# A fused stage with a one-group TensorE loop and single buffers, and row sums written for every row of O in layer 0

## The reference, cut to what matters

```python
def _attn(q_in, k_in, v_in, wq, bq, wk, bk, wv, bv, wo, bo, causal):
    Q = (q_in @ wq + bq).reshape(Bq, Sq, H, HD)
    Kp = (k_in @ wk + bk).reshape(Bq, Sk, H, HD)
    V = (v_in @ wv + bv).reshape(Bq, Sk, H, HD)
    scores = jnp.einsum('bqhd,bkhd->bhqk', Q, Kp) / jnp.sqrt(jnp.float32(HD))
    ...
    a = jax.nn.softmax(scores, axis=-1)
    o = jnp.einsum('bhqk,bkhd->bqhd', a, V).reshape(Bq, Sq, Dm)
    return o @ wo + bo
...
x = _layernorm(x + _attn(x, x, x, ..., True), ln1_g, ln1_b)                             # "sa"
x = _layernorm(x + _attn(x, encoder_output, encoder_output, ..., False), ln2_g, ln2_b)  # "ca"
x = _layernorm(x + _moe(x, ...), ln3_g, ln3_b)
# layer 1: attention of _layer_norm(x) over _layer_norm(context), x + out, then the MLP
```

## Time and profile before

| | |
|---|---|
| three runs | 1499.0, 1501.34, 1504.86 us (median 1501.34) |
| the profiled execution | 1501.08 us, span 1499.4 us |
| layers sa and ca | about 14 to 560 us |
| routing, experts | to about 944 us |
| fused stage | about 947 to 1357 us |
| MLP | to the end |
| PE busy / granted clock over the span | 86% / 0.933 of full speed |

### The profile page before, as it was taken

One profiled execution on the slowest core, in us unless ns is written; L12 is line 12 of the kernel. 1 busy time (PEld: TensorE's weight loads), 2 busy tenths in 40 slices (PEclk: granted clock), 3 DMA queues, 4 the chain that ended last, 5 costly groups with the idle time before them and its releaser, 6 DMA issues. The chain is left out here.

```text
span 1499.4 us, 59843 instructions
## 1 busy us (share of the span) xinstructions
PE 1284.4 (86%) x23136; PEld 1073.3 (72%) x23136; DVE 969.2 (65%) x2107; ACT 997.0 (66%) x2030; POOL 861.9 (57%) x1340
## 2 busy tenths in 40 slices
PE   5999999989999987679999999157887777895998
PEld 2787887778888776568999999136665556683776
DVE  4787787767878865883555555266877767762332
ACT  1778877768788852986666666166776666772554
POOL 2557766656676753108999987566555554322331
PEclk9999999999999995598999999669999999996999
DMA  3232332322322430522222223242332323212221
GB/s 102 76 103 91 98 105 91 95 87 80 89 80 88 117 90 8 176 64 63 69 68 68 68 67 65 66 106 65 84 89 68 96 64 82 66 31 57 71 70 49
DMA packets 154923, 118.91 MB, mean 79 GB/s; under 512 B 17440, under 2 KB 130592, under 8 KB 154784
## 3 DMA queue, kind: packets, MB, share of 16 engines
q1 hardware_dynamic: 146336, 99.61, 22.6%
q0 software_dynamic: 8448, 17.32, 5.1%
HBM read 78.55 MB, written 38.27 MB: 78 GB/s over the span
## 5 line engine op out<-in xcount | busy, mean ns | idle before, releaser
L831 DVE TENSOR_REDUCE at_mx<-at_ps_s 128x16 f32<-128x1024 f32 x128 | 156.1, 1220 | 106.9 <-PE at_ps_s L560 60.4
L760 ACT ACTIVATE at_pt<-at_ps_t 128x1024 f32<-128x1024 f32 x128 | 130.6, 1020 | 56.3 <-PE at_ps_t L574 55.6
L753 ACT ACTIVATE at_pr<-at_dd 128x1024 f32<-128x1024 f32 x128 | 135.2, 1056 | 34.7 <-DVE at_dd L839 34.6
L2261 ACT ACTIVATE ex_hg<-ex_ps_h,ex_wt 128x128 f32<-128x128 f32 x544 | 154.4, 372 | 1.3 <-PE ex_ps_y L2230 1.2
L2201 POOL DMA_INDIRECT ex_xg<-x,ex_ti x136 | 141.2, 1038 | 23.4 <-issue 21.8
L2282 DVE COPY ex_wt<-experts 128x1156 f32 x136 | 105.0, 774 | 75.7 <-issue 64.3
L839 DVE TENSOR_TENSOR at_dd<-at_ps_s,at_mx 128x1024 f32<-128x1024 f32 x128 | 153.8, 1203 | 0.1
L2221 PE MATMUL ex_ps_h<-ex_xt,ex_wt 128*128 128x128 f32 x1088 | 148.6, 281 | 0.0
L1611 POOL DMA_INDIRECT l_yg<-rows,l_sl x128 | 128.8, 1007 | 33.0 <-issue 30.8
L574 PE MATMUL at_ps_t<-ident,at_pr 128*128 128x128 f32 x1024 | 139.9, 280 | 5.1 <-issue 3.1
L2230 PE MATMUL ex_ps_y<-ex_wt,ex_hg 128*128 128x128 f32 x1088 | 143.6, 275 | 0.4 <-ACT ex_hg L2261 0.4
(11 more groups left out here) (239 smaller groups left out, 3282.9 us busy)
## 6 DMA issues: line engine op xcount, KB each, us to landing
rows<-ex_y SPq DMA_DIRECT2D x136, 64.0 KB
x<-at_ln_out SPq DMA_DIRECT2D x32, 256.0 KB, 3.2
at_kx<-in_xt SPq DMA_DIRECT2D x16, 256.0 KB, 2.8
at_qx<-in_xt SPq DMA_DIRECT2D x16, 256.0 KB, 2.8
at_vin<-in_xt SPq DMA_DIRECT2D x16, 256.0 KB, 2.7
at_xr<-in_x SPq DMA_DIRECT2D x16, 256.0 KB, 3.0
x1t<-at_xt SPq DMA_DIRECT2D x16, 256.0 KB, 3.2
at_kx<-in_ctxt SPq DMA_DIRECT2D x16, 256.0 KB, 2.7
```

The costliest lines, as they stand in the source:

```text
L753: act.activation(pr[:, p], dd[:, p], ACT.Exp, scale=SCALE).then_inc(p_ready, 1)
L760: act.activation(pt[:, 2 * h + p], ps_t[:, :, :, :], ACT.Copy).then_inc(pt_ready, 1)
L831: dve.tensor_reduce(mx[:, p], ps_s[:, :, 4 * p:4 * p + 4, :], AX.X, ALU.max).then_inc(mx_ready, 1)
L2261: ins = act.activation(hg[:, s % 2, f, :], ps_h[s % HB][:, f, :], ACT.Gelu, bias=wt[:, s % HB, B1 + f:B1 + f + 1])
```

## The change

In `attention_phase`, `values` now multiplies by `c.count_all`, a block with ones for every row of a head, and writes the sums of sequence b beside its O, to columns 256 + 64 b onward. All 256 columns come out as row sums, and DVE inverts all of them and multiplies O by them straight from PSUM. `copy_o`, `spread` and `widen` are gone there, with their tiles and semaphores. `fused_phase` keeps `recip` of 64 columns, `spread`, `copy_o` and `widen`.

In `fused_phase` the PE program runs `over_ones`, a loop over one group (groups 2 to 14), and `kv`, `qx`, `kb`, `qb`, `c.vx`, `ot`, `z4` have one buffer each; `kv` is split into `kx` and `vin`, loaded apart. PE projects k one group ahead, and v in the group's own step, ahead of the next group's first scores. The orders on PE, ACT, DVE, POOL and SP are turned so that a step starts at another place, and a few neighbours are exchanged.

```diff
@@ attention_phase @@
-        rc = n.sb("rc", [P, 2, SEQ])
-        rcx = n.sb("rcx", [P, 2, QB, SEQ])
-        ov = n.sb("ov", [P, 2, GT // 2])
+        rc = n.sb("rc", [P, 2, GT // 2])
...
                             for r in range(4):
-                                mm = pe.matmul(ps_o[32 * r:32 * r + 32, GT // 2:GT // 2 + SEQ],
-                                               c.count[:, b, f, :],
+                                mm = pe.matmul(ps_o[32 * r:32 * r + 32,
+                                                    GT // 2 + SEQ * b:GT // 2 + SEQ * b + SEQ],
+                                               c.count_all[:, 24 * f:24 * f + 32],
                                                pt[:, 2 * h + b // 2, b % 2, r, SEQ * f:SEQ * f + SEQ],
                                                start=False, stop=(b == QB - 1 and f == 1), skip_group_check=True)
...
-                    if prior:
-                        widen(g * 2 - 2, 0)
...
-                    if prior:
-                        copy_o(g * 2 - 2, 0)
...
                 def recip(quad, h):
                     dve.wait_ge(pv_ready, quad + 1)
-                    if beyond(quad, 1):
-                        dve.wait_ge(rcx_ready, quad - 1)
-                    dve.reciprocal(rc[:, h, :], ps_o[:, GT // 2:GT // 2 + SEQ]).then_inc(rc_ready, 1)
+                    dve.reciprocal(rc[:, h, :], ps_o[:, GT // 2:GT]).then_inc(rc_ready, 1)
 
                 def normalise(a, h):
                     quad = a.g * 2 + h
-                    dve.wait_ge(r_ready, quad + 1)
+                    dve.wait_ge(rc_ready, quad + 1)
                     if beyond(a.g, 0):
                         dve.wait_ge(o_ready, a.g)
-                    dve.wait_ge(ov_ready, quad + 1)
-                    dve.tensor_tensor(ot[:, GT // 2 * h:GT // 2 * h + GT // 2], ps_o[:, GT // 2:GT], ov[:, h, :],
+                    dve.tensor_tensor(ot[:, GT // 2 * h:GT // 2 * h + GT // 2], ps_o[:, 0:GT // 2], rc[:, h, :],
                                       ALU.mult).then_inc(ot_ready, 1)
...
-                    if prior:
-                        spread(g * 2 - 2, 0)
@@ fused_phase @@
-        kv = n.sb("kv", [P, 2, GT])
-        qx = n.sb("qx", [P, 2, GT])
+        kx = n.sb("kx", [P, GT])
+        vin = n.sb("vin", [P, GT])
+        qx = n.sb("qx", [P, GT])
...
                 def step(a):                                   # SP
-                    if a.shift(2).exists():
-                        load_kv(a.shift(2))
                     if a.shift(1).exists():
                         load_x(a.shift(1))
                     if a.shift(-2).exists():
                         store_tok(a.shift(-2))
-                    if a.shift(5).exists():
-                        load_front(a.shift(5))
+                    if a.shift(4).exists():
+                        load_front(a.shift(4))
                     if a.shift(3).exists():
                         store_x3(a.shift(3))
+                    if a.shift(2).exists():
+                        load_k(a.shift(2))
+                    if a.shift(1).exists():
+                        load_v(a.shift(1))
...
-                over_steps(pe, step, NG - 2)
+                over_ones(pe, step, -1, NG - 1, NG + 2)
...
                 def mask_k(a):
                     act.wait_ge(k_ready, a.g + 1)
-                    if beyond(a.g, 1):
-                        act.wait_ge(s_ready, 2 * a.g - 2)
+                    if beyond(a.g, 0):
+                        act.wait_ge(s_ready, 2 * a.g)
```

More of the change, by code:

```diff
@@ L597, in values @@
                     mm.then_inc(pv_ready, 1)
[L599 to L603, removed]
                 def project_k(a):
@@ L955, in mask_q @@
                     ins.then_inc(qb_ready, 1)
[L957 to L960, removed]
-                    pool.tensor_tensor(rcx[:, h], rc[:, h, None, :].broadcast_to([P, QB, SEQ]),
-                                       c.own[:, :, None].broadcast_to([P, QB, SEQ]), ALU.mult).then_inc(rcx_ready, 1)
                 def add_bias(a):
@@ L1006, in _ @@
                 last = At(nl, NG * nl - 1)
-                spread(last.g * 2, 0)
                 if closing:
@@ L1010, in _ @@
                     gain(last.shift(-1))
-                spread(last.g * 2 + 1, 1)
                 context.pool_rstd(pool, c, 0, 0)
@@ L1087, in fused_phase @@
         z4t_ready, qx_ready = n.sem("z4t_ready"), n.sem("qx_ready")
-        in_kv = [n.sem(f"in_kv{i}") for i in range(2)]
+        in_k, in_v = n.sem("in_k"), n.sem("in_v")
         in_x = [n.sem(f"in_x{i}") for i in range(2)]
@@ L1219, in project_k @@
                 def project_k(a):
-                    pe.wait_ge(in_kv[a.u], 16 * (a.k + 1))
-                    pe.matmul(ps_g[:, :], layer.wk[:, :], kv[:, a.u, :], start=True, stop=True).then_inc(
+                    pe.wait_ge(in_k, 16 * a.g + 16)
+                    pe.matmul(ps_g[:, :], layer.wk[:, :], kx[:, :], start=True, stop=True).then_inc(
                         k_ready, 1)
@@ L1225, in project_q @@
                     pe.wait_ge(qx_ready, a.g + 1)
-                    pe.matmul(ps_g[:, :], layer.wq[:, :], qx[:, a.u, :], start=True, stop=True).then_inc(
+                    pe.matmul(ps_g[:, :], layer.wq[:, :], qx[:, :], start=True, stop=True).then_inc(
                         q_ready, 1)
                 def project_v(a):
-                    pe.wait_ge(in_kv[a.u], 16 * (a.k + 1))
+                    pe.wait_ge(in_v, 16 * a.g + 16)
                     w = layer.wv[:, :].rearrange("p (r j m) -> p r j m", r=4, j=2)
@@ L1241, in project_out @@
                     for t in range(GP):
-                        mm = pe.matmul(ps_g[:, D * t:D * t + D], ot[:, a.u, P * t:P * t + P], layer.wo[:, :],
+                        mm = pe.matmul(ps_g[:, D * t:D * t + D], ot[:, P * t:P * t + P], layer.wo[:, :],
                                        start=True, stop=True)
@@ L1253, in step @@
                     g = a.g
+                    if a.shift(-2).exists():
+                        if a.shift(-1).exists():
+                            pe.wait_ge(vx_ready, g)
+                        else:
+                            pe.wait_ge(y_ready, g - 2)
+                        project_out(a.shift(-2))
+                    if a.shift(-1).exists():
+                        turn(g * 2 - 1, 1, 1)
+                    if a.exists():
+                        scores(a, 1)
                     if a.shift(1).exists():
@@ L1651, in step @@
                     if a.shift(-1).exists():
[L1652 removed]
                         add_bias(a.shift(-1))
+                    if a.shift(4).exists():
+                        fetch(a.shift(4), 0, 1)
+                        fetch(a.shift(4), 1, 2)
+                        fetch(a.shift(4), 2, 3)
+                    if a.shift(-1).exists():
+                        spread(g * 2 - 1, 1)
+                    if a.shift(4).exists():
+                        fetch(a.shift(4), 3, 4)
+                        fetch(a.shift(4), 4, 5)
                 pool.wait_ge(bob_ready, 1)
```

182 lines of the change are left out of this document (77 added, 105 removed).

## The result

| | before | after | ratio, 95% interval |
|---|---|---|---|
| median, 20 runs each | 1506.47 us | 1498.91 us | 0.9937 [0.9914, 0.9959] |
| the profiled execution | 1501.1 us | 1501.5 us | |

The change makes the kernel 0.6% faster. 1455 us was predicted, with a range of 1435 to 1487, so the time lies outside it.

The account below looks back on a forecast made before the run. PE's instruction fetches, queued with gathers, were taken to stall the fused stage. From 1501.1 us, -55.8 (fused loop), +3.5 (single buffers) and +6 (layers sa and ca) gave 1454.8, predicted as 1455 us, range 1435 to 1487.

Parts of the forecast that it names:

- What bounds the kernel: Fused stage: PE waits 35.2 us for its own instructions, from a too long body and gathers its refills queue with.
- The step of 17.0 us a group: Last fused loop step, after the gathers end: 13 blocks fetched, yet 17.01 us a group, so fetching alone costs little.
- The fused loop, -55.8: Fused stage: the halved body ends the fetches, nine periods fall from 24.0 to 17.8 us, 55.8 us off.
- the floor of 17.8: Fused loop: DVE bounds next, 17.7 us a group fully packed; period taken as 17.8 us.
- The old body is longer than one that fits: PE's fused loop: the new body of 809 records is shorter than a fitting 844; the old 1618 does not fit.
- Layers sa and ca, +6: Attention layers: DVE becomes the bound, groups get 0.1 and 0.2 us longer, 6 us added in all.
- The reciprocal: DVE in layers sa and ca: 256 columns instead of 64 take 1.73 us, +1.18 each, +2.36 a group.
- the wait that stays: DVE in layer sa: 1.58 us a group idle before the next quad's maximum cannot be filled; about 1.25 in ca.
- overlap of about 0.08 each: DVE in layers sa and ca: three waits that go give back about 0.08 us each, 0.25 a group.
- Single buffers, +3.5: Fused stage: k's mask shows at the start (+1.5 to 2) and in three last groups (0.5 each), +3.5 us.
- Serial chain: Rival, fused stage: `load_k` behind `store_x3` brings k late, period 20 us, 36 saved, total 1474.5 us; chance 0.16.
- Fetches persist: Rival, fused loop: the body is still refetched, period stays 24.0 us, only losses remain, 1510.6 us; chance 0.07.

Follow-up runs that it names:

- before_direct_sp: The kernel before with each fused-stage gather replaced by a plain load of 128 fixed rows issued by SyncE: 1440.5 us, 0.996 of before, calm occasion.
- after_again: The changed kernel, unaltered, measured again beside the kernel before on a calm occasion: 1441.5 us against 1449.0, ratio 0.9957.
- fused_only: The new fused stage with the old layers sa and ca: 1433.4 us, 0.992 of before (calm); 1495.5 us, 0.9841 (stalled).
- attn_only: The new layers sa and ca with the old fused stage: 1442.5 us, 0.9976 of before, calm occasion.
- pad_late: The kernel before with 39 small matmuls ahead of PE's fused loop, behind a wait for `bob_ready`: 1492.6 us against 1512.0, 0.9872, stalled occasion.
- after_b: The changed kernel, unaltered, measured again beside the new fused stage alone on a stalled occasion: 1509.1 us, 0.9947 of before.

## Why the prediction was wrong

**What bounds the kernel: two stalls taken for one.** The step that failed is the reading of the earlier trace rows: 35.2 us of issue waits, all "PE waiting for its own instructions", made of "a body too long to stay in place, and gathers that its refills queue with". 9.8 us of them, at the head of the body, were refills, and those need no gathers. The 25.4 us in `values` were for the most part something else: with one block moved in 216 us, 22.9 remain. They come mostly while POOL is at a gather, only on some occasions, and go when SyncE loads the rows. The pieces are also not all of 0.4 us: L1207 in the earlier trace rows has one of 1.8, and three of 1.3 to 1.8 us, 4.7 together, fall where POOL is at no gather and are of the size that the eight-block body shows without gathers, so this part of the 25.4 is more likely refills too. The step of 17.0 us a group in the earlier trace rows could not show what fetching costs. It starts right behind the 3.35 us of the head, which come once in two groups, so it holds none of them, and it has no gathers. In `before_direct_sp`, without gathers, the steps that hold the head take 22 to 24 us and the others 18 to 19.

**The fused loop, -55.8.** Where the stalls in `values` are absent the mechanism is right; its term was too large everywhere. The refills are gone, and the floor of 17.8 that I took from DVE fully packed is the 17.5 of the calm occasion, DVE 99% busy and the clock at 1.00. But refills cost 2.2 us a group on a calm occasion (19.8 us in nine periods); on the stalled one the periods went only from 24.0 to 22.7, 12 us of the 55.8. From the end of `ex_y` to that of the last residual the first two traces have 410.4 and 403.7 us: 6.7 less, where -55.8 and +3.5 stood in the sum. The layers' +10.7, and 3.6 us less in the other stages, make up the +0.4 between these traces.

**"The old body is longer than one that fits."** Length alone does not decide. The same 1663 instructions moved nine blocks a pass over 8 blocks, and over 7 none after the first pass. The Trainium skill, "Runtime: NRT & Kernel Launch", section "Instruction fetch mechanics", gives PE 2048 instructions in blocks of 256 refilled one after the other, and has a taken branch to a block outside its window of two stall. I had set the page aside, because 1618 is below 2048 and yet 38 blocks moved. The runs agree with its room for eight blocks, with one step more: a body over eight moved nine in every pass and lost its head each time, at 4 us (11.5 us in three), and one over seven stayed. If the ninth is the block behind the body, fetched ahead, seven and one fit in eight and eight and one do not; which blocks moved, no run shows. With a window of two the runs disagree: the branch back over seven blocks waited for nothing.

**Layers sa and ca, +6.** Measured 10.7 to 13.6. The reciprocal was right (1.748 against 1.73 us), DVE as the bound too, and the wait that stays (1.6 us, 14.4 in nine groups). The mis-sized term is the "overlap of about 0.08 each" that I credited, 0.25 us a group: 32 groups of it are 8 us. Without it the prediction's own sums give 16.53 and 16.17 us a group and 12 us for the layers; the groups take 16.56 in sa and 16.19 in ca. From the repeat count of 8 that the Trainium skill gives in "VectorE: DVE Perf Modes", section "Walkthrough: the 8-slice pipeline in each mode", an estimate of 2.15 us followed; the trace disagrees with its 1.748.

**Single buffers, +3.5.** On the calm occasion the second `turn_z` comes 17.85 us after the first instead of 16.0, as forecast; in the middle they cost nothing that shows (waits of PE for `l_kb` 1.1 us in six groups). As a whole the new fused stage, 339.9 us in `after_again` and 341.4 in `fused_only`, is 2.4 to 3.9 us longer than the old one with its body over seven blocks (337.5 in `attn_only`), which is about the term.

**The rivals.** "Serial chain" did not come: no wait for `l_kx`. "Fetches persist" was wrong in its mechanism, since the blocks are gone, and near in its time: a stall that the body does not cause keeps the period close to 24. The range left it out because I gave all of the earlier trace rows one cause.

**Where the gain is.** On a calm occasion: -20.2 us in the fused stage, +11.8 from the attention part, together -8.4; the medians differ by -7.4. The -20.2 are the refills less what the new stage costs, for the old stage with its body over seven blocks is 22.6 us shorter than over eight (337.5 and 360.1). So the gain can be had without the new stage, by moving the old body. The best versions are `fused_only` (0.992 calm, 0.984 stalled) and `pad_late` (0.987 stalled); they were not run side by side.

## What to carry to other kernels

Split a wait labelled "issue" by the line and the length of its pieces before giving it one cause: 4 us at the first instruction of a body and 0.4 us inside dense small matmuls were different things. Check a loop body's place as well as its length, by the instruction blocks moved in a pass that is not the first; 156 idle instructions in front of the loop were worth 1.3% on the one occasion where they stood at a place where nobody waits. Where the engine that becomes the bound is lengthened, take no credit for overlaps that no row shows.

## What the hardware showed that was not expected

The same kernel on the same chip (5) took 1515 us on one occasion and 1448 on another. In the traces of the stalled kind the fused stage is 50 to 73 us longer; layers, routing, experts and MLP agree within a few us, but for `after_b`, where `ex_y` ends 9 us later than in `after_again`. The granted clock does not set the two apart: over six groups of before it is 0.94 on the stalled occasion and 0.93 on the calm one. The gathers themselves are no slower: POOL takes 0.99 us for one on average in the first trace of the changed kernel and 1.00 in `after_again`. And 39 matmuls of a single column took 16.8 us, 0.43 each.
